# Attention kernel on graphs: key term of the second layer added to the mask by POOL, and the third layer's fold put in the batch's own accumulator

## The reference, cut to what matters

```python
# layer 1: additive attention
h = relu(fa[:, :, None, :] + fb[:, None, :, :]); att = einsum('bijo,o->bij', h, W2)
x = softmax(att + mask) @ feat
# layer 2: the same form with a leaky ReLU (slope 0.2) and a linear layer behind it
lr = leaky(vu[:, :, None, :] + iv[:, None, :, :]);  scores = einsum('bijc,c->bij', lr, yita)
scores = where(adj > 0, scores, -1e12);  alpha = softmax(scores, axis=2)
# layer 3: softmax over the rows of each column
logits = leaky(f1[:, None, :] + f2[:, :, None], 0.01)
coefs = softmax(where(adj > 0, logits, -9e15), axis=1);  ret = elu(coefs @ seq_fts)
# layer 4: 8-head attention with a bias by edge type
```

## Time and profile before

| | us |
|---|---|
| median of three runs | 6055.87 |
| the profiled execution | 6059.57 |
| its span (first to last instruction) | 6057.8 |
| PE busy | 5889.8 (97%) |
| DVE busy | 5202.7 (86%) |
| ACT busy | 5284.7 (87%) |
| POOL busy | 649.8 (11%) |
| layers 1 and 2, from the first to the last `masked_min` | 59.8 to 4018.6 |
| layer 3, the 64 `masked_max` | 4068.6 to 4275.9 (their first and last start) |

### The profile page before, as it was taken

One profiled execution on the slowest core, in us unless ns is written; L12 is line 12 of the kernel. 1 busy time (PEld: TensorE's weight loads), 2 busy tenths in 40 slices (PEclk: granted clock), 3 DMA queues, 4 the chain that ended last, 5 costly groups with the idle time before them and its releaser, 6 DMA issues. The chain is left out here.

```text
span 6057.8 us, 131997 instructions
## 1 busy us (share of the span) xinstructions
PE 5889.8 (97%) x53828; PEld 2701.6 (45%) x53828; DVE 5202.7 (86%) x8890; ACT 5284.7 (87%) x6081; POOL 649.8 (11%) x441
## 2 busy tenths in 40 slices
PE   8999999999999999999999999987799999999999
PEld 2333333333333333333333333334577766767766
DVE  8999999999999999999999999966577777777777
ACT  8999999999999998999989899967588888888887
POOL 0000000000000000000000000003212112112111
PEclk9999999999999999999999999988799999999999
DMA  1000000000000000000000000015100000000000
GB/s 40 19 19 19 19 19 19 19 19 19 19 19 19 19 15 19 19 19 15 19 19 19 15 19 19 15 48 150 48 23 24 20 24 24 20 24 24 20 24 10
DMA packets 109656, 147.66 MB, mean 24 GB/s; under 512 B 16966, under 2 KB 84294, under 8 KB 109062
## 3 DMA queue, kind: packets, MB, share of 16 engines
q1 hardware_dynamic: 108422, 139.15, 7.3%
q10 hardware_dynamic: 640, 0.07, 0.0%
HBM read 137.10 MB, written 2.10 MB: 23 GB/s over the span
## 5 line engine op out<-in xcount | busy, mean ns | idle before, releaser
L257 ACT ACTIVATE a_hidden<-a_B,a_A 128x1024 f32<-128x1024 f32 x3200 | 3435.4, 1139 | 288.1 <-PE apsS L211 284.4
L333 DVE TENSOR_SCALAR a_hidden<-a_B,a_A 128x1024 f32<-128x1024 f32 x4992 | 3481.7, 767 | 199.6 <-PE apsS L211 174.3
L211 PE MATMUL apsS<-a_hidden,a_w_sel 128*32 128x512 f32 x32768 | 3563.1, 594 | 2.8 <-DVE a_hidden L333 2.8
L211 PEld LDWEIGHTS apsS<-a_hidden,a_w_sel 128*32 128x32 f32 x32768 | 1045.4, 110 | 2407.4 <-issue 2023.3
L703 ACT ACTIVATE Z<-m3S,bias 128x1024 f32<-128x1024 f32 x512 | 569.7, 1113 | 307.2 <-PE m3S L646 307.2
L753 DVE CUSTOM_DVE_ANT_0 Z<-Z,mask 128x1024 f32<-128x1024 f32 x512 | 624.9, 1221 | 120.8 <-ACT Z L703 118.9
L766 DVE COPY PT<-m3T 128x512 f32<-128x512 f32 x512 | 354.1, 692 | 319.7 <-PE m3T L658 319.2
L658 PE MATMUL m3T<-ident,Z 128*128 128x128 f32 x4096 | 565.4, 279 | 42.9 <-DVE PT L766 41.1
L711 ACT ACTIVATE Z<-Z,negm 128x1024 f32<-128x1024 f32 x512 | 588.8, 1150 | 12.5 <-DVE negm L759 12.5
L658 PEld LDWEIGHTS m3T<-ident,Z 128*128 128x128 f32 x4096 | 440.9, 141 | 283.5 <-issue 275.8
L121 POOL TENSOR_SCALAR a_mask<-a_adj_in 128x1024 f32<-128x1024 int32 x128 | 181.1, 1415 | 3426.4 <-DVE small L342 2951.2
(11 more groups left out here) (163 smaller groups left out, 2681.7 us busy)
## 6 DMA issues: line engine op xcount, KB each, us to landing
a_adj_in<-adj SPq DMA_DIRECT2D x128, 512.0 KB, 3.3
adj_in<-adj SPq DMA_DIRECT2D x128, 512.0 KB, 3.9
out<-yn SPq DMA_DIRECT2D x64, 32.0 KB, 1.5
x_even<-x SPq DMA_DIRECT2D x1, 256.0 KB, 2.8
wqT<-L_wqT SPq DMA_DIRECT2D x1, 130.0 KB, 2.5
wkT<-L_wkT SPq DMA_DIRECT2D x1, 130.0 KB, 2.7
wvT<-L_wvT SPq DMA_DIRECT2D x1, 130.0 KB, 2.8
wp<-L_gnn_Wp SPq DMA_DIRECT2D x1, 128.0 KB, 2.8
```

The source lines that it names most:

```text
L211: last = pe.matmul(psS[k % 2][32 * q:32 * q + 32, h * HALF:(h + 1) * HALF], w["sel"][layer][:, 30 - 2 * p:62 - 2 * p], hidden[:, (k * GROU ...
L257: act.activation(hidden[:, (k * GROUPS + p) % SLOTS, q, :], B2[:, g % 2, :], ACT.Relu, bias=A2[:, g % 2, pair:pair + 1]).then_inc(hid_act, 1)
L333: dve.tensor_scalar(hidden[:, (k * GROUPS + p) % SLOTS, q, :], B2[:, g % 2, :], A2[:, g % 2, pair:pair + 1], 0.0, ALU.add, ALU.max).then_i ...
```

## The change

**Layer 2.** The jobs `key_term` and `turn_t`, the DVE split and the two matmuls for each tile are gone. `w["u"]` holds the key vector in 128 equal columns, so that one matmul for each half (job `key_rows`, new L169) gives the key term of 512 keys on all 128 partitions. ACT copies it to a new buffer `TB`. For each tile of layer 2 POOL makes the mask as before, waits for its own instruction, and then adds `TB` to the mask in place (a new `tensor_tensor` of 128 x 1024 fp32, new L131). `AHEAD` has seven entries in place of eight: the two `key_rows` stand at (4, 1) and (5, 0). The first hidden matmul of a tile starts the accumulator in both layers.

**Layer 3.** `fold_halves` writes into the accumulator `psR[b % 2]` of the batch itself, which has been copied out by then, and stands at j = 6 in place of 7. Its waits for the use of `psA` go, those of `turn_x` too. The first `weigh` of a batch waits until the fold of the batch two before has been read.

```diff
-    AHEAD = {(0, 0): 0, (0, 1): 1, (1, 0): 2, (1, 1): 3, (2, 1): 4, (4, 1): 5, (6, 0): 6, (6, 1): 7}
+    AHEAD = {(0, 0): 0, (0, 1): 1, (1, 0): 2, (1, 1): 3, (2, 1): 4, (4, 1): 5, (5, 0): 6}
...
+                m, row = k - nb * tiles, k // tiles % 2
+                if m < 0:
+                    gp.tensor_scalar(mask[:, k % 2, :], adj_in[:, k % 2, :], NEG, -NEG, ALU.mult,
+                                     ALU.add).then_inc(mask_ready, 1)
+                    return
                 gp.tensor_scalar(mask[:, k % 2, :], adj_in[:, k % 2, :], NEG, -NEG, ALU.mult,
-                                 ALU.add).then_inc(mask_ready, 1)
+                                 ALU.add).then_inc(mask_made, 1)
+                if m % tiles == 0:
+                    gp.wait_ge(aux_out, done("key_rows", k // tiles, 1))
+                gp.wait_ge(mask_made, m + 1)
+                gp.tensor_tensor(mask[:, k % 2, :], mask[:, k % 2, :], TB[:, row, :], ALU.add).then_inc(mask_ready, 1)
...
-                elif what == "key_term":
-                    for t in range(tiles):
-                        last = pe.matmul(psA[:, t:t + 1], B2[0:C, g % 2, t * P:(t + 1) * P], w["u"], start=True, stop=True)
-                elif what == "turn_t":
-                    pe.wait_ge(t_split, g - nb + 1)
-                    pe.nop(nofuse=True)
-                    for t in range(4):
-                        last = pe.transpose(psA[0:3, t * P:(t + 1) * P], tsplit[:, 4 * i + t, :], ident)
+                elif what == "key_rows":
+                    last = pe.matmul(psA[:, :], w["u"], B2[0:C, g % 2, i * HALF:(i + 1) * HALF], start=True, stop=True)
...
-                                         start=p == 0 and layer == 0, stop=p == GROUPS - 1)
+                                         start=p == 0, stop=p == GROUPS - 1)
...
-                        if nb * tiles <= k + 1 < K:
-                            add_key_term(k + 1)
...
-                    if p == 7 and j == 5 and nb <= g + 1 < G:
-                        split_key_term(g + 1 - nb)
...
                 pe.wait_ge(seq_scaled, k + 2)
                 if j == 0 and b >= 2:
-                    pe.wait_ge(ret_out, b - 1)
+                    pe.wait_ge(neg_ready, b - 1)
+                    pe.wait_ge(pos_ready, b - 1)
...
             def fold_halves(b):
                 pe.wait_ge(ret_out, b + 1)
-                pe.wait_ge(seq_out, min(b + 3, nb))
-                if b >= 1:
-                    pe.wait_ge(neg_ready, b)
-                    pe.wait_ge(pos_ready, b)
                 for t in range(tiles):
-                    last = pe.matmul(psA[:, t // 4, t % 4 * C:(t % 4 + 1) * C], ret[:, t * P:(t + 1) * P], fold,
+                    last = pe.matmul(psR[b % 2][:, t * C:(t + 1) * C], ret[:, t * P:(t + 1) * P], fold,
                                      start=True, stop=True)
...
-                if j == 7 and 0 <= b - 1 < nb:
+                if j == 6 and 0 <= b - 1 < nb:
                     fold_halves(b - 1)
```

More of the change, by code:

```diff
@@ L51, in additive_layers @@
     adj_in, mask, Z, PT, OT, y = buf["adj_in"], buf["mask"], buf["Z"], buf["PT"], buf["OT"], buf["y"]
-    tcol, thigh, tsplit, T3 = buf["tcol"], buf["thigh"], buf["tsplit"], buf["T3"]
+    TB = buf["TB"]
     stats, mv, vare, rstd, den, rden = (buf[s] for s in ("stats", "mv", "vare", "rstd", "den", "rden"))
@@ L63, in projection @@
         jobs = [("turn_x", g, 0), ("turn_x", g, 1), ("keys", g, 0), ("keys", g, 1), ("queries", g, 0)]
-        return jobs + ([("key_term", g, 0), ("turn_t", g, 0), ("turn_t", g, 1)] if g >= nb else [])
+        return jobs + ([("key_rows", g, 0), ("key_rows", g, 1)] if g >= nb else [])
     def finishing(g):
         return [("fold", g, 0)] + ([("turn_u", g, 0), ("turn_u", g, 1), ("linear", g, 0)] if g >= nb else [])
-    AHEAD = {(0, 0): 0, (0, 1): 1, (1, 0): 2, (1, 1): 3, (2, 1): 4, (4, 1): 5, (6, 0): 6, (6, 1): 7}
+    AHEAD = {(0, 0): 0, (0, 1): 1, (1, 0): 2, (1, 1): 3, (2, 1): 4, (4, 1): 5, (5, 0): 6}
     BEHIND = {(2, 0): 0, (3, 0): 1, (3, 1): 2, (4, 0): 3}
@@ L273, in aux @@
                     act.activation(A2[:, g % 2, :], psA[:, :], ACT.Copy).then_inc(aux_out, 1)
[L274 to L279, removed]
+                elif what == "key_rows":
+                    if g >= nb + 2:
+                        act.wait_ge(mask_ready, (g - 1) * tiles)
+                    act.activation(TB[:, g % 2, half], psA[:, :], ACT.Copy).then_inc(aux_out, 1)
                 else:
@@ L349, in copy_high @@
                 dve.tensor_copy(PT[:, HALF:n], psT[:, HALF:n]).then_inc(copied_high, 1)
[L351 to L365, removed]
             def scale(g):
@@ L456, in _ @@
             dve.tensor_scalar(w["sel"][1], w["sel"][1], GAT_SLOPE - 1.0, None, ALU.mult)
-            dve.tensor_scalar(w["u"], ycol, -GAT_SLOPE, None, ALU.mult)
+            dve.tensor_scalar(w["u"], ycol.to_broadcast([C, P]), -GAT_SLOPE, None, ALU.mult)
             dve.tensor_scalar(w["beta1"], w["beta1"], 1.0, None, ALU.add)
             dve.tensor_tensor(w["fold"], w["ident"][:, 0:C], w["ident"][:, C:P], ALU.add)
-            dve.memset(w["ones"], 1.0)
 HEADS = 8
@@ L885, in build @@
                        mask=sg("a_mask", [P, 2, n]), Z=sg("a_Z", [P, n])[:, :], PT=sg("a_PT", [P, n]),
-                       OT=sg("a_OT", [P, tiles, P])[:, :, :], y=sg("a_y", [P, tiles * C])[:, :], tcol=sg("a_tcol", [P, tiles])[:, :],
-                       thigh=sg("a_thigh", [P, 2, tiles], BF16), tsplit=sg("a_tsplit", [P, tiles, 3]),
-                       T3=sg("a_T3", [3, 2, n], BF16), stats=sg("a_stats", [P, tiles, 6]), mv=sg("a_mv", [P, tiles, 2]),
+                       OT=sg("a_OT", [P, tiles, P])[:, :, :], y=sg("a_y", [P, tiles * C])[:, :], TB=sg("a_TB", [P, 2, n]),
+                       stats=sg("a_stats", [P, tiles, 6]), mv=sg("a_mv", [P, tiles, 2]),
                        vare=sg("a_vare", [P, tiles])[:, :], rstd=sg("a_rstd", [P, tiles])[:, :],
@@ L892, in build @@
             w_a, w_b = [sg(f"a_w_a{i}", [C, 2, P]) for i in range(2)], [sg(f"a_w_b{i}", [C, P]) for i in range(2)]
-            u, lin_w, lin_b, beta = sg("a_u", [C, 1]), sg("a_lin_w", [C, C]), sg("a_lin_b", [P, C]), sg("a_beta", [P, 1])
-            ycol, fold, ones = sg("a_ycol", [C, 1]), sg("a_fold", [P, C]), sg("a_ones", [3, P], BF16)
+            u, lin_w, lin_b, beta = sg("a_u", [C, P]), sg("a_lin_w", [C, C]), sg("a_lin_b", [P, C]), sg("a_beta", [P, 1])
+            ycol, fold = sg("a_ycol", [C, 1]), sg("a_fold", [P, C])
             xv = a["x"].rearrange("(t p) c -> p t c", p=P)
@@ L908, in build @@
             w = dict(a=w_a, b=[t[:, :] for t in w_b], sel=[t[:, :] for t in w_sel], u=u[:, :], lin=lin_w[:, :],
-                     lin_b=lin_b[:, :], beta1=beta[:, :], fold=fold[:, :], ones=ones[:, :], ident=ident[:, :])
+                     lin_b=lin_b[:, :], beta1=beta[:, :], fold=fold[:, :], ident=ident[:, :])
             additive_constants(nc, w, ycol[:, :])
@@ L1088, in turn_x @@
                     pe.wait_ge(seq_out, b)
-                if b >= 3:
-                    pe.wait_ge(neg_ready, b - 2)
-                    pe.wait_ge(pos_ready, b - 2)
                 pe.nop(nofuse=True)
@@ L1201, in positive_part @@
                     dve.wait_ge(written, b)
-                dve.scalar_tensor_tensor(out=y.rearrange("p (h c) -> p h c", h=2), in0=psA[:, :, 0:4 * C], scalar=0.0,
-                                         in1=X[:, b * tiles * C:(b + 1) * tiles * C].rearrange("p (h c) -> p h c", h=2),
+                dve.scalar_tensor_tensor(out=y, in0=psR[b % 2][:, 0:tiles * C], scalar=0.0,
+                                         in1=X[:, b * tiles * C:(b + 1) * tiles * C],
                                          op0=ALU.max, op1=ALU.add).then_inc(pos_ready, 1)
@@ L1288, in negative_part @@
                     act.wait_ge(y_ready, b)
-                act.activation(neg.rearrange("p (h c) -> p h c", h=2), psA[:, :, 0:4 * C], ACT.Relu,
+                act.activation(neg, psR[b % 2][:, 0:tiles * C], ACT.Relu,
                                scale=-1.0).then_inc(neg_ready, 1)
```

2 lines of the change are left out of this document (1 added, 1 removed).

## The result

| | before | after |
|---|---|---|
| median of the runs | 6057.03 us (4 runs) | 6015.01 us (4 runs, 6011.74 to 6019.70) |
| ratio, 95% interval | | 0.9929 [0.9912, 0.9946] |
| span of the profiled execution | 6057.8 | 6009.9 |
| layer 1, first to last minimum | 1924.4 | 1925.0 |
| layer 2, last minimum of layer 1 to its own last | 2034.4 | 2001.3 |

The change is 0.7% faster, 42 us by the medians and 47.9 by the two spans. Of the spans' 47.9, layer 2 gives 33.1 and layer 3 14.0. The rest, layer 4 above all, took 2.0 longer. The prediction was 6011.

A forecast was written before the change was run, and what follows sets the result against it. PE was taken to bound layer 2, DVE close behind, and the chain of waits layer 3. Gains of 30 + 15 = 45 us off 6059.6 gave 6014.6, predicted as a 6011 us median; the forecast's own range was 5997 to 6034.

The forecast's parts named there:

- PE's need: Layer 2: PE's time for a batch of 8 tiles, 255.4 - 4.2 - 2.9 + 2.1 = 250.4 us, 5.0 less than before.
- 28.4 us a tile and 7.4 for the batch steps: Layer 2: DVE's need without the add and the key term's split, 227.4 + 7.4 = 234.8 us a batch.
- d: Layer 2: DVE time lost to each POOL add, by one hidden instruction being held up; taken as 2.05 us.
- 0.4 for unevenness: Layer 2: 0.4 us a batch added to DVE's 251.2, as DVE and PE don't meet evenly: 251.6.
- either bound: Layer 2: limits for the add's cost to DVE, the mask's 0.79 us below and POOL's longest two-input instruction, 2.55, above.
- a middle: Layer 2: 2.05 us for the add's cost to DVE, between twice the mask's push, 1.58, and 2.5.
- The first rival: Layer 2: the add costs DVE under 1.6 us, PE is the bound, gain 40 + 15, total 6001; chance 0.15.
- The slow rival: Layer 2: the add costs DVE 3.3 us, DVE needs 261.6 a batch, kernel slower by 35 at 6091; chance 0.12.
- the one at 2.5 to 2.8: Layer 2: the add costs DVE 2.5 to 2.8 us, layer 2 gives -2 to +18, total 6039 to 6059; chance 0.15.
- ACT's own wait: Layer 3: ACT's 7 waits for the fold, 15.4 us in total, taken as the gain of 15, bounds 0 and 18.
- The rival that the wait passes on: Layer 3 gives nothing: the time saved is waited for at the next tile, or the fold delays the mask's turn; 6026; chance 0.14.
- the predicted 3.8: Layer 2: gain of a batch, from 255.4 to 251.6 us; over eight batches 30 us.

The follow-up runs named there:

- no_add: The whole change without POOL's add, so the key term is made but left out of layer 2's scores: 5998.75 us, ratio 0.9905 to before.
- share26: The whole change with ACT making 26 of a tile's 64 hidden tensors in place of 25, and DVE 38, in both layers: 5998.05 us, ratio 0.9903 to before.
- half_add: The whole change with POOL's add over the first 512 keys only, the key term of the others left out: 5997.74 us, one time.
- add_twice: The whole change with a second POOL add of the same size for each layer 2 mask, into a spare buffer: 6150.78 us, one time.
- l3_only: Only the third layer's part of the change, with layer 2's code as in the kernel before: ratio 0.9978 to before.
- fold_j7_own: The whole change with layer 3's fold in its own accumulator with the new waits, but still at j = 7: 6032.09 us, one time.

## Why the prediction was right

**Layer 2, PE.** PE's need was predicted as 250.4 us a batch; without the add it is 249.75. The terms themselves were read rightly. What the sum lacks stands in the timelines of PE (`before` and `no_add`). With no key-term matmuls behind it, the `turn` takes 0.93 us until the next job starts at three places of a batch (2738.01 to 2738.94 in `no_add`), where it takes 1.02 in the kernel before (2756.85 to 2757.87), and these three jobs are 0.03 to 0.10 us shorter too. And the two `turn_t` and the `key_term` broke a tile's run of hidden matmuls twice a batch, the `key_rows` do it once: two runs of 128 take 0.14 more than one of 256 (2 x 13.87 against 27.60). That makes some 0.6 of the 0.65. The error stayed hidden as long as DVE was the bound, and showed in `no_add` and `share26`, whose gains I put at half their size.

**Layer 2, DVE.** Its need was built from single durations, 28.4 us a tile and 7.4 for the batch steps, with d = 2.05 and 0.4 for unevenness: 251.6. Measured is 251.3, with d = 2.13. So the sum without d is 251.3 - 8 x 2.13 = 234.3 against 234.8, and the 0.4 was not needed. That step decided what layer 2 was forecast to gain: DVE's busy share of 93% alone would have given 255.4 x 0.93 = 238 us a batch, 255 with the add, and next to no gain there. An estimate from the Trainium skill, "GPSIMD Engine Reference", section 3.1, had given d = 2.0; the measured 2.13 is nearer to it than to either bound.

**What the text called a middle** between 1.58 and 2.5 was a guess about a loop over two streams; that 2.05 came so near to 2.13 was luck in part. `half_add` and `add_twice` turn it into a rate. The first rival (the add is cheap) had L129 for it, whose 8 elements held up nothing; it falls with `add_twice`. The slow rival (d = 3.3) and the one at 2.5 to 2.8 fall with the same row.

**Layer 3.** 15 us were predicted from ACT's own wait, 14.0 measured. The 15.4 hold a seventh wait of 2.1 behind the last maximum, which both kernels have; the six in front of it were 13.3 and are gone. The rival that the wait passes on falls. The reason was right as well: the idle time of PE in front of the turned mask.

**Not in the sum.** Layer 2 of the kernel before had three stretches at 1.2 GHz, 3.4 us each, that the prediction left out. The busy row of the first, and the matmuls around it:

```profile
2377.70:2381.20 3.50, 3.50 (x20) 0.87 (x16) 1.61 (x3) 0.47 (x1) 0.00 (x0) 0.51 0.00 0
```

```profile
2374.89 0.60 PE L223 MATMUL apsS<-a_T,a_ones 3*128 3x512 bf16 x2
2375.42 2.00 PE L174 MATMUL apsA<-a_lin_w,a_uT 64*128 64x64 f32 x16
2377.34 13.06 PE L211 MATMUL apsS<-a_hidden,a_w_sel 128*32 128x512 f32 x104
```

The granted clock is 0.51 in it. It comes right behind the key-term matmuls and the linear layer. PE does half its work there, 1.7 us lost each time, some 5 us in all. `l3_only`, the one experiment with the key-term matmuls, has one such stretch, and none of the profiles without them has any in layer 2. That these matmuls bring it about is likely, but no run separates them from the rest of the change.

**What cancelled.** The 33.1 us of layer 2 are not 8 times the predicted 3.8. The middle batches gained 4.1 each, but the first one 2.8 and the last two 2.8 and 2.0, so without the clock it is 28.0, two less than the 30; the 5.1 of the three stretches make it 33.1. `l3_only` agrees, as it has two stretches fewer in an unchanged layer 2 and is 3.4 us shorter there. The 2.8 of the gap between the layers and the 2.0 lost elsewhere were no part of the sum either. The mechanism was right, but that the total came within 4 us of 6011 owes something to luck.

## What to carry to other kernels

An instruction moved to an idle engine is not free when the engine that is second in line shares something with it: look for the one instruction of that engine that is longer than its fellows, and take its excess as the price. Build the second engine's need from instructions that run freely, not from its busy share, which its waits inflate; here the busy time gives 238 us a batch and the need is 234.3; some 0.9 of the difference is the key term's split, which goes, and the other 3 us, times eight, are most of layer 2's gain. In a pipeline of engines walking one index, a step's place in the list can cost more than the step: look for the idle time in front of which it could stand.

## What the runs showed of the hardware

- A two-input add of 128x1024 fp32 on POOL takes 2.69 us beside DVE's hidden instructions and holds one of them up by 2.13; 128x512 takes 1.60 and holds one up by 1.03. The one-input mask of 128x1024 takes 1.42 and costs 0.79.
- The hidden instruction that is held up ends 0.54 to 0.56 us behind the end of POOL's mask or add, in all 190 cases of the kernel after (126 masks and 64 adds), and in `half_add` and `add_twice` as well. So a large POOL instruction holds DVE until it is over.
- The hold-up follows the elements, not the length of the instruction: the power of 128x8 (2.55 us on POOL) held up nothing. The Trainium skill, "SBUF — State Buffer", section "SBUF: two separate sides", has the loser blocked for the whole instruction; the runs agree for the large ones, by the ends above, and disagree for this small one.
- In layer 3 the fold took 1.95 to 2.0 us at a granted clock of 1.00 (kernel after) and 3.68 inside stretches at 0.50 (`fold_j7_own`), and ACT's wait for it grew from at most 2.9 to 3.88 us.
